# How the last group of an attention kernel shares its projection matmuls out over its slots

## The reference, cut to what matters

```python
x = x + 0.5 * ffn(layernorm(x))
x = x + attn(layernorm(x))      # 32 query heads, 8 key/value heads, width 128, window 128
x = x + 0.5 * ffn(layernorm(x))

def attn(x):
    q, k, v = x @ wq, x @ wk, x @ wv
    q, k = rope(q), rope(k)
    p = softmax(mask(q @ k.T * scale))
    return (p @ v) @ wo
```

## Time and profile before

| | |
|---|---|
| median of 3 runs | 727.90 us (727.89 to 728.08) |
| the profiled execution's own time | 728.14 us |
| its span, first to last instruction | 726.4 us |
| TensorE busy | 714.5 us, 98% of the span |
| granted TensorE clock, mean | 1.000 |
| group 7, first half | 613.56 to 649.99 us |
| group 7, last half | from 649.99 us |

### The profile page before, as it was taken

One profiled execution on the slowest core, in us unless ns is written; L12 is line 12 of the kernel. 1 busy time (PEld: TensorE's weight loads), 2 busy tenths in 40 slices (PEclk: granted clock), 3 DMA queues, 4 the chain that ended last, 5 costly groups with the idle time before them and its releaser, 6 DMA issues.

```text
span 726.4 us, 13750 instructions
## 1 busy us (share of the span) xinstructions
PE 714.5 (98%) x3699; PEld 603.5 (83%) x3699; DVE 522.3 (72%) x1773; ACT 424.3 (58%) x1146; POOL 396.5 (55%) x515
## 2 busy tenths in 40 slices
PE   8999989999999999999999999999999999999998
PEld 6887768888888888888888888888888888887886
DVE  6778776767777777677776677676767776778784
ACT  3456675556664675557655766476657665655440
POOL 2365676535853496447743765368535864374630
PEclk9999999999999999999999999999999999999999
DMA  8140013000310022002100120003000310030002
GB/s 274 56 166 29 0 39 93 15 0 8 100 40 2 0 77 68 1 1 73 58 15 1 58 73 15 1 28 103 15 2 0 102 29 0 1 117 1 0 31 88
DMA packets 25870, 32.34 MB, mean 45 GB/s; under 512 B 5834, under 2 KB 14282, under 8 KB 25300
## 3 DMA queue, kind: packets, MB, share of 16 engines
q1 hardware_dynamic: 25232, 30.69, 13.4%
q10 hardware_dynamic: 580, 1.05, 0.4%
HBM read 27.55 MB, written 4.19 MB: 44 GB/s over the span
## 4 chain that ended last, share of the span: by engine, by line
PE 88%; DVE 4%; POOL 4%; ACT 1%; issue 1%; DMA 1%; SPq 0%; DVEq 0%; POOLq 0%; ACTq 0%
PE bank L1192 33%; PE bank L1253 24%; PE bank L1235 8%; PE bank L1214 7%; PE bank L1153 4%; PE bank L1222 4%; PE bank L1211 2%; POOL wo_lo L405 1%; PE bank L1175 1%; PE bank L1201 1%; PE bank L1212 1%; DVE stats L789 1%; PE bank L1138 1%; PE bank L1126 1%; PE bank L1143 1%
## 5 line engine op out<-in xcount | busy, mean ns | idle before, releaser
L413 POOL TENSOR_TENSOR swap<-swap,rope 128x512 f32<-128x512 f32 x80 | 104.5, 1307 | 116.3 <-ACT swap L593 115.8
L420 POOL TENSOR_SCALAR_AFFINE_SELECT pT_hi_lo<-pT_hi_lo 128x256 fp32r<-128x256 f32 x128 | 52.4, 409 | 140.4 <-DVE pT_hi_lo L943 140.4
L619 ACT ACTIVATE bank<-sm,nmax 128x128 f32<-128x128 f32 x128 | 47.6, 372 | 105.1 <-DVE nmax L928 105.0
L627 ACT ACTIVATE pT_hi_lo<-bank 128x256 fp32r<-128x256 f32 x128 | 49.2, 385 | 95.1 <-PE bank L1222 62.8
L593 ACT ACTIVATE swap<-bank 64x512 f32<-64x512 f32 x160 | 95.1, 594 | 15.0 <-PE bank L1192 12.5
L943 DVE TENSOR_TENSOR pT_hi_lo<-bank,pT_hi_lo 128x256 fp32r<-128x256 f32 x128 | 53.8, 420 | 52.5 <-ACT pT_hi_lo L627 52.2
L430 POOL TENSOR_TENSOR q_lo<-rot,q_hi 128x512 fp32r<-128x512 f32 x64 | 82.7, 1293 | 1.3 <-ACT q_hi L601 1.3
L1253 PE MATMUL bank<-wo_hi,oT_hi 128*128 128x512 f32 x256 | 74.6, 413 | 0.0
L1192 PE MATMUL bank<-xnT_lo,wq_hi 128*128 128x512 f32 x256 | 73.3, 389 | 0.0
L894 DVE TENSOR_TENSOR rot<-bank,rope 128x512 f32<-128x512 f32 x80 | 55.1, 689 | 25.2 <-ACT swap L593 25.1
L1192 PE MATMUL bank<-xnT_hi,wq_hi 128*128 128x512 f32 x256 | 71.9, 393 | 1.0 <-DVE v_lo L914 0.8
(11 more groups left out here) (158 smaller groups left out, 1695.2 us busy)
## 6 DMA issues: line engine op xcount, KB each, us to landing
raw<-in_L_attn_wq SPq DMA_DIRECT2D x32, 256.0 KB, 2.9
raw<-in_L_attn_wo SPq DMA_DIRECT2D x32, 256.0 KB, 2.7
x<-in_L_attn_x SPq DMA_DIRECT2D x4, 512.0 KB, 7.4
raw<-in_L_attn_wk SPq DMA_DIRECT2D x8, 256.0 KB, 2.6
raw<-in_L_attn_wv SPq DMA_DIRECT2D x8, 256.0 KB, 2.6
out<-x SPq DMA_DIRECT2D x8, 256.0 KB, 2.0
raw<-in_L_ffn_W_base ACTq DMA_DIRECT2D x4, 256.0 KB, 5.3
wb_keep_hi<-q_hi SPq DMA_DIRECT2D x1, 1024.0 KB, 4.9
```

Of the source, the lines that this page charges most:

```text
L413: nc.gpsimd.tensor_tensor(w, w, tab, ALU.mult).then_inc(t2_done, 1)
L420: nc.gpsimd.affine_select(pT_both[:, :, 2, h, :], pT_both[:, :, 1, h, :].bitcast(F32), pattern=[[0, 2], [1, P]], compare_op=ALU.is_ge, fil ...
```

## The change

In the last group, the first half's slots hold 9, 9, 9, 9, 9, 5, 5 and 5 projection matmuls instead of 8 and 7 in turns (60 in both cases), and the 12 matmuls of V stand in slot 0 of the last half instead of 6 in slot 0 and 6 in slot 1. As `ended` follows from it, the steps of rope and of V move between slots on all engines.

```diff
--- before.py
+++ after.py
@@ -48,7 +48,7 @@
 
 CHUNKS = (9,) * SLOTS
 FIRST_HALF = (12, 12, 12, 12, 6, 6, 6, 6)
-LAST_HALVES = ((8, 7, 8, 7, 8, 7, 8, 7), (6, 6, 0, 0, 0, 0, 0, 0))
+LAST_HALVES = ((9, 9, 9, 9, 9, 5, 5, 5), (12, 0, 0, 0, 0, 0, 0, 0))
 
 
 def spread(first, last, hf):
```

## The result

The changed kernel takes 729.79 us (median of 9, 729.52 to 730.15) against 727.96 us before (median of 9, 727.84 to 728.15). The ratio is 1.0025, with a 95% interval of 1.0017 to 1.0033: 1.8 us slower. The prediction said 729.5 us, in a range of 728.4 to 730.3.

The account below looks back on a forecast made before the run. TensorE, busy 98% of the span, was taken as the bound, so only its waits could matter; 2.29 us of delay less 0.12 and 0.56 us of slack gave +1.61, from 727.90 to 729.5 us, range 728.4 to 730.3.

Parts of the forecast that it names:

- Step 1, the wait for wo: First half, slot 6: TensorE waits 1.07 us for wo's lo part against 0.66 before, +0.41 us.
- Step 1, slot 7: First half, slot 7: TensorE waits 0.19 us for DVE's addition to x to free the output projection's bank.
- Step 2: V in one slot: V's wait goes (-1.63 us), but waits of 0.6 and 0.7 us come in slots 1 and 2.
- longer chain: Last half: x's statistics on DVE and POOL, then ACT's normalisation and exponentials, delay the first dense matmul by 1.61 us.
- Step 3: Last half: x's statistics come 2.29 us later; less slack, the first dense matmul moves by +1.61 us.
- P: Start of the probabilities' transposes in slot 0 of the last half, 651.93 us in the kernel before.
- two slacks: Last half: 0.12 us before ACT's normalisation and 0.56 us before its slot 3 exponentials, taken off the delay.
- the last stretch: Last half: from ACT's slot 3 exponentials over DVE's queue to the first dense matmul, 4.11 us, taken as unchanged.
- the bound of what can be told: Whole kernel: a measurement tells a change from none at about 0.2%, 1.46 us.
- The case that only moved the wait: Rival, last half: the wait only changes its place, +0.3 us, 728.2 us, no measurable change; chance 0.13.
- the faster one: Rival, last half: only V's wait goes and the softmax keeps up, 726.3 us, 726.9 with step 1; chance 0.05.
- The slower one: Rival, first half: splits still take 5.52 us (+0.48) or softmax falls behind (up to 0.4), 730.0 to 730.4 us; chance 0.12.

Follow-up runs that it names:

- run 1: The kernel before with only the new first half (9, 9, 9, 9, 9, 5, 5, 5), V left in two pieces of 6: 728.71 us.
- run 6: The kernel before with the first half's slots at 8, 7, 7, 6, 6, 9, 9, 8, so slots 5 and 6 are long: 727.16 us.
- run 2: The kernel before with only V moved, 12 matmuls in slot 0 of the last half, old first half: 728.95 us.
- run 3: The changed kernel with DVE's statistics of x's first two tiles taken in slot 0 ahead of the probabilities' lo part: 728.90 us.
- run 4: The kernel before with V's difference made ahead of the probabilities' lo part in slot 1 of the last half: 727.58 us.

## Why the prediction was right

**Step 1, the wait for wo.** Predicted 1.07 us, measured 1.05; the lo parts took 5.03 us where the prediction took 5.04. The relation read from group 6 carried over to a half that shares its first five slots. The stretched 5.52 us did not recur here, nor in runs 1 and 6 (5.03 and 5.05), where DVE's rope sum stands clear of the splits; in run 2, which keeps the old places, it is 5.48 us. The Trainium skill (SBUF — State Buffer, Who interferes with whom) has it that such a pair contends and that the later of the two is blocked. The trace of before agrees: the sum starts at 637.80, while POOL's first split runs, and takes 1.37 us for 0.68; the split that follows takes 1.79 us, the other three 1.28 to 1.32.

**Step 1, slot 7.** Predicted 0.19 us, measured 0.30. The mechanism was right and the size off: DVE's addition ended at 647.50 (row below: 646.82 + 0.68), and TensorE started 0.15 us behind it where 0.04 had been put in for the release. The trace of before had such a release: the transposes at 98.04 start 0.15 us behind DVE's lo part. DVE in slots 6 and 7:

```profile
644.76 0.87 DVE L903 TENSOR_TENSOR rot<-rot,swap 128x512 f32<-128x512 f32 x1 [1.33 <-POOL swap L413]
...
646.82 0.68 DVE L956 TENSOR_TENSOR x<-bank,x 128x512 f32<-128x512 f32 x1
```

**Step 2.** Waits of 0.6 and 0.7 us were predicted for slot 1's transposes and slot 2's scores, and the starts show 0.6 (655.20, where slot 0's pattern from 653.79, 0.14 + 0.58 us and 0.1 for the restart of the scores, gives 654.6) and 0.70 (658.59, 1.06 us behind V's transposes where 0.36 would do). In the changed kernel they lie under the longer chain, as predicted. Once the chain is out of the way, slot 1's wait comes to light (run 3). The transposes of x waited 0.50 us for the first tile, 0.6 predicted, and again between the tiles.

**Step 3.** POOL's start was put at P + 4.24 and was P + 4.24; the dense matmul at 17.6 us behind the last half's first, and came at 17.64. Inside, one of two slacks was misread. Of the 0.17 us between POOL's end and ACT's start the prediction took only 0.05 for the release, and 0.12 to be saved; but with ACT idle for 1.26 us they are still 0.16 us (662.45 to 662.61). It is the time of the release, and no slack. The slack before the exponentials was put at 0.56 us and was 0.57 (ACT starts them 1.43 us behind the normalisation's start when nothing else holds them, 662.61 to 664.04; before, it took 2.00 us).

**The sum.** Predicted +1.61 us; measured in the trace +1.77, and in the medians +1.83. Term by term: P comes 2.04 us later against the group's start (1.96 predicted), V's difference adds 0.33 (0.33), the two slacks take 0.01 and 0.57 (0.12 and 0.56), and the last stretch gives 0.02 (0): 1.77. The two mis-sized terms, slot 7's wait (0.11 more) and the slack that is a release (0.11 less), went the same way; some hundredths in the other terms went against them. The forecast stood only 0.15 us past the bound of what can be told, and gave 0.40 to "within 0.2%"; the result is 0.25%. The case that only moved the wait is refuted by runs 2 and 3, the faster one by run 2. The slower one had two conditions, and neither came: the lo parts took 5.03 us, and in the first half from 613 us on TensorE waits only for wo's lo part and the 0.30 us of slot 7.

## What to carry to other kernels

A wait of the bounding engine is worth its length only up to the next thing that is late. Here 1.5 us of waiting for V could be removed for a gain of 0.3 us (run 4), or for a loss of 1.1 us (run 2), depending on what was moved ahead of the next hand-over. When work is moved ahead of an engine's hand-over (here slot 0's scores and transposes), list everything that other engines start from that hand-over, down to the latest consumer, before counting the wait that goes. Where one handed-out amount of work covers several latencies, put it where the longest one stands (with 18 matmuls in slots 5 and 6, TensorE came 8.90 us behind slot 4's transposes, for lo parts ready at 8.10), not evenly and not early. And before covering a late result, see why it is late: here 0.72 of the 8.82 us came from rope steps that the same tuples had put in its way.

## What the runs showed of the hardware

The release from one engine to the next is not one number. Waits of TensorE fall into two kinds in these traces. Lo parts on POOL to the second pass took 0.05 us (643.50 to 643.55), and V's difference to its transposes, in the kernel before, 0.06 us (657.82 to 657.88). DVE's addition to TensorE's next output projection took 0.15 us (647.50 to 647.65), probabilities to scores 0.15 (658.44 to 658.59), the lo part to slot 1's transposes 0.15 (655.05 to 655.20), and x's lo part to the first dense matmul 0.14 (667.99 to 668.13). In the kernel's code a single wait stands ahead of the two short ones, and two or more in a row ahead of the four long ones. POOL's last statistics step to an idle ACT, also behind several waits, took 0.16 us. Whether the number of waits is the reason was not tried.

A rope sum on DVE and a POOL split that met both took longer, 1.37 us for 0.68 and 1.79 for 1.28, and the four splits with them 5.52 instead of 5.03 us. They release TensorE, so by the rows this one meeting held it back by almost 0.5 us.
